# First attention of a two-layer kernel: the first two heads' convolution matrix loaded straight from a padded input, D added on its diagonal by VectorE

## The reference

```python
# head_dim 8, 16 heads over the 128 rows of the sequence axis, L = 256
kv = einsum('bhil,bhjl->bijhl', k_, v_)            # k = v = ctx
y = irfft(rfft(kv, 2L) * rfft(ssm_kernel, 2L))[..., :L]   # causal convolution along L
out = y + kv * D[None, None, None, :, None]
out = einsum('bijhl,bhil->bjhl', out, q_)          # q = layernorm(x)
x = x + out
```

## Time and profile before

| | |
|---|---|
| median of 3 runs | 797.25 us (795.12 to 798.29) |
| profiled execution, its own time | 793.92 us |
| span from its first to its last instruction | 792.2 us |
| mean granted TensorE clock | 0.960 of full speed |
| busy: PE, DVE, ACT, POOL | 709.6, 543.6, 342.7, 443.1 us |

### The profile page before, as it was taken

The page is one execution under the profiler, slowest core; times in us unless marked ns, Lnnn a source line. Parts: engine busy times, 40 slices in busy tenths (PEclk is TensorE's granted clock), DMA queues, the critical chain, the costliest instruction groups (busy, mean ns, idle before and its releaser), DMA issues.

```text
span 792.2 us, 14732 instructions
## 1 busy us (share of the span) xinstructions
PE 709.6 (90%) x5217; PEld 648.2 (82%) x5217; DVE 543.6 (69%) x1278; ACT 342.7 (43%) x698; POOL 443.1 (56%) x532
## 2 busy tenths in 40 slices
PE   4899978949999981769899999999999999999996
PEld 2444557839999970658899999999999999999996
DVE  4999988786666655676667677677676586755533
ACT  2564533235666652264354344344444534443221
POOL 5877955047666605565276466474664773443532
PEclk9999999978999995689999999999999999999998
DMA  7675516936866763414012021010020110000000
GB/s 252 191 175 123 140 41 144 195 89 194 234 197 195 164 151 125 141 54 146 1 35 61 1 60 36 14 54 28 15 67 14 34 49 1 2 14 2 2 14 14
DMA packets 44599, 68.67 MB, mean 87 GB/s; under 512 B 7376, under 2 KB 32240, under 8 KB 44528
## 3 DMA queue, kind: packets, MB, share of 16 engines
q0 software_dynamic: 10080, 28.72, 16.3%
q1 hardware_dynamic: 34352, 38.97, 15.2%
q10 hardware_dynamic: 96, 0.04, 0.0%
HBM read 50.77 MB, written 14.84 MB: 83 GB/s over the span
## 4 chain that ended last, share of the span: by engine, by line
PE 52%; DVE 4%; POOL 3%; ACT 2%; issue 2%; POOLq 0%; DVEq 0%
PE psum L1428 19%; PE psum L1413 9%; PE psum L1460 9%; PE psum L1474 4%; PE psum L1446 2%; PE psum L1510 2%; PE psum L1500 2%; PE psum L1487 2%; POOL rows_back L1699 1%; PE psum L1528 1%; PE psum L1548 1%; DVE lora_w_lo L1794 1%; PE psum L1518 1%; ACT lora_w_hi L1592 0%; POOL hid L1719 0%
## 5 line engine op out<-in xcount | busy, mean ns | idle before, releaser
L1719 POOL TENSOR_TENSOR hid<-hid,rw_sb 128x256 f32<-128x256 f32 x112 | 93.3, 833 | 153.1 <-DVE hid L1919 152.8
L1428 PE MATMUL psum<-am_hi,lora_w_hi 128*128 128x256 f32 x448 | 127.4, 284 | 2.6 <-DVE am_lo L1914 2.3
L1428 PE MATMUL psum<-am_hi,lora_w_lo 128*128 128x256 f32 x448 | 127.2, 284 | 0.0
L1428 PE MATMUL psum<-am_lo,lora_w_hi 128*128 128x256 f32 x448 | 127.1, 284 | 0.0
L1919 DVE TENSOR_TENSOR hid<-hid,psum 128x256 f32<-128x256 f32 x112 | 46.7, 418 | 116.5 <-ACT hid L1599 115.3
L1599 ACT ACTIVATE hid<-psum 128x256 f32<-128x256 f32 x112 | 42.4, 385 | 177.1 <-PE psum L1428 176.9
L1022 POOL DMA_INDIRECT rows_in<-y_scratch,slot_token x80 | 76.3, 954 | 36.0 <-issue 27.3
L1428 PEld LDWEIGHTS psum<-am_hi,lora_w_hi 128*128 128x128 f32 x448 | 86.0, 192 | 3.1 <-POOL am_lo L1730 3.1
L1699 POOL DMA_INDIRECT rows_back<-slots_scratch,comb_idx x64 | 67.1, 1049 | 37.0 <-POOLq L707 21.4
L1925 DVE TENSOR_TENSOR hid_lo<-hid,hid_hi 128x256 fp32r<-128x256 f32 x112 | 74.0, 681 | 19.3 <-ACT hid_hi L1605 14.4
L1428 PEld LDWEIGHTS psum<-am_lo,lora_w_hi 128*128 128x128 f32 x448 | 85.9, 192 | 0.0
(11 more groups left out here) (255 smaller groups left out, 2137.4 us busy)
## 6 DMA issues: line engine op xcount, KB each, us to landing
slots_scratch<-y_out SPq DMA_DIRECT2D x40, 256.0 KB, 2.5
stage<-in_moe_weights SPq DMA_DIRECT2D x18, 384.0 KB, 3.8
moe_w_lo<-in_moe_weights POOLq DMA_DIRECT2D x18, 384.0 KB, 6.5
lora_stage_early<-in_lora_weights SPq DMA_DIRECT2D x16, 384.0 KB, 3.3
x_sb<-in_x SPq DMA_DIRECT2D x4, 512.0 KB, 6.1
ctx_t<-in_ctx_t SPq DMA_DIRECT2D x4, 512.0 KB, 7.3
y_scratch<-y SPq DMA_DIRECT2D x8, 256.0 KB, 2.6
x_sb<-shared_out POOLq DMA_DIRECT2D x4, 512.0 KB, 5.2
```

Of the source, the lines that this page charges most:

```text
L1428: last = nc.tensor.matmul(x_banks[F % 2][:, w * GT:(w + 1) * GT], wp, ap, start=False, stop=(half == 1 and k == 2), skip_group_check=True)
L1719: nc.gpsimd.tensor_tensor(f[:, F % 2, k, :], f[:, F % 2, k, :], rw_sb[:, F // FB % 2, k, :], ALU.mult)\
```

## The change

The input `ssm_kernel` is padded on the host to the form of `kpad`, so that the Toeplitz block of a head can be read from it directly, without D. Part 0 (heads 0 and 1) is read in this way and no longer waits for the store; its load stands in SP's queue between the two loads of x. Parts 1 and 2 still come from `kpad_scratch`, with D in them. For heads 0 and 1 DVE adds D itself: `first_tap` is a 128 x 128 matrix with ones where the first tap stands in the block (POOL makes it: a memset and an `affine_select`), `d_first` is D of the two heads on all 128 partitions (a third DMA in ACT's queue), and two `scalar_tensor_tensor` instructions write first_tap * D + toeplitz over the block. PE's step 0 now waits for these two. POOL's two memsets of `kpad` are gone. The padded row is loaded whole (24 KB in place of 16 KB).

```diff
+    DIRECT = 2
...
-    TOEPLITZ_PARTS = ((0, 2), (2, HEADS // 2), (HEADS // 2, HEADS))
+    TOEPLITZ_PARTS = ((0, DIRECT), (DIRECT, HEADS // 2), (HEADS // 2, HEADS))
...
-                sp.dma_start(toeplitz[:, first:end, :], bass.AP(kpad_dram.tensor, first * KPAD, [
+                source = a["ssm_kernel"] if part == 0 else kpad_dram
+                sp.dma_start(toeplitz[:, first:end, :], bass.AP(source.tensor, first * KPAD, [
...
             load_x(0)
+            load_toeplitz(0)
             load_x(1)
             load_context(0)
             sp.wait_ge(kpad_stored, 16)
-            load_toeplitz(0)
             load_toeplitz(1)
...
-            nc.gpsimd.memset(kpad[:, 0:P - 1], 0.0)
-            nc.gpsimd.memset(kpad[:, P - 1 + DIM:KPAD], 0.0).then_inc(kpad_zero, 1)
             nc.gpsimd.memset(ident[:, :], 0.0).then_inc(ident_done, 1)
             nc.gpsimd.memset(minus_half[:, :], -0.5)
+            nc.gpsimd.memset(first_tap[:, :], 0.0).then_inc(tap_done, 1)
...
+            pool.wait_ge(tap_done, 1)
+            nc.gpsimd.affine_select(out=first_tap[:, :], in_=first_tap[:, :], compare_op=ALU.not_equal, fill=1.0,
+                                    base=1 - P, pattern=[[1, P]], channel_multiplier=1).then_inc(tap_done, 1)
...
-            act.dma_start(kpad[:, P - 1:P - 1 + DIM], a["ssm_kernel"]).then_inc(k_loaded, 16)
+            act.dma_start(kpad[:, :], a["ssm_kernel"]).then_inc(k_loaded, 16)
             act.dma_start(d_col[:, :], a["D"]).then_inc(k_loaded, 16)
-            act.wait_ge(kpad_zero, 1)
+            act.dma_start(d_first[:, :], a["D"][0:DIRECT, :].rearrange("h o -> (h o)").partition_broadcast(P))\
+               .then_inc(toeplitz_loaded[0], 16)
             act.wait_ge(d_added, 1)
...
-                        pe.wait_ge(toeplitz_loaded[part], 16)
+                        if part == 0:
+                            pe.wait_ge(direct_ready, DIRECT)
+                        else:
+                            pe.wait_ge(toeplitz_loaded[part], 16)
...
-            for p in range(DVE_ROWS):
-                query_rows(p)
+            query_rows(0)
+            query_rows(1)
+            dve.wait_ge(toeplitz_loaded[0], 32)
+            dve.wait_ge(tap_done, 2)
+            for h in range(DIRECT):
+                own_block = toeplitz[:, h, 0:P]
+                nc.vector.scalar_tensor_tensor(own_block, first_tap[:, :], d_first[:, h:h + 1], own_block, ALU.mult,
+                                               ALU.add).then_inc(direct_ready, 1)
+            query_rows(2)
```

More of the change, by code:

```diff
@@ L175, in first_phase @@
         prod = sb("prod", [P, HALVES * CHUNK_B, HEAD_DIM, HEAD_DIM])
-        with nc.sbuf_tensor("kpad", [HEADS, KPAD], FP32) as kpad:
+        with nc.sbuf_tensor("kpad", [HEADS, KPAD], FP32) as kpad, \
+                nc.sbuf_tensor("first_tap", [P, P], FP32) as first_tap, \
+                nc.sbuf_tensor("d_first", [P, DIRECT], FP32) as d_first:
             pass
@@ L189, in sem @@
             return s.enter_context(nc.semaphore(name))
-        kpad_zero, k_loaded, d_added, kpad_stored = map(sem, ("kpad_zero", "k_loaded", "d_added", "kpad_stored"))
+        tap_done, k_loaded, d_added, kpad_stored = map(sem, ("tap_done", "k_loaded", "d_added", "kpad_stored"))
+        direct_ready = sem("direct_ready")
         toeplitz_loaded = [sem(f"toeplitz_loaded{i}") for i in range(len(TOEPLITZ_PARTS))]
@@ L2068 @@
         "ctx_t": ctx_rev.transpose(1, 2, 0),
-        "ssm_kernel": inputs["L0_xattn_ssm_kernel"],
+        "ssm_kernel": np.pad(np.asarray(inputs["L0_xattn_ssm_kernel"]), ((0, 0), (P - 1, KPAD - DIM - P + 1))),
         "moe_gate": np.asarray(inputs["L0_ffn_gate_weight"]).T.reshape(HALVES, P, EXPERTS).transpose(1, 0, 2),
```

## The result

The changed kernel takes 799.07 us in the median of 22 runs (794.03 to 801.67), the kernel before 796.76 us (794.79 to 800.37, 22 runs). The ratio is 1.0021, 95% interval 1.0011 to 1.0031: slower by 1.7 us (0.9 to 2.5; the two medians lie 2.3 us apart), inside the 0.5% that were set as "no change", and clear of zero.

What follows compares the result with a forecast made beforehand. DVE's pace was taken to bound the step loop, so the start chain from D's landing to its first product counts; removed wait 0, additions 0, x and context 0, D +0.3 gave 797.5 us, range 794.5 to about 800.6.

Steps and rivals of the forecast that it cites:

- forecast as summed: Whole kernel: +0.3 us, to 797.5 us, with a band of -0.3 to +0.8 us; chance 0.63.
- the case "same": Whole kernel: the time changes by under 0.5% (4 us); chance 0.92, against faster 0.03 and slower 0.05.
- rival (a): DVE before pair 2: additions miss the idle hole, pair 2 waits behind POOL's kv; 0.4 to 2.5 us, likely 1.4; chance 0.22.
- The removed wait, 0: PE's step 0: Toeplitz part 0 already landed 1.8 us before PE wanted it, so dropping its wait for the store gains 0.
- DVE's additions, 0: DVE before pair 2: the two additions, 0.29 us each, fit the 0.62 us idle while POOL computes its power; cost 0.
- x and context, 0: SP's queue: the block delays x tiles 4 to 7 and the context by 1.2 us (bound 1.9), hidden by slack; cost 0.
- D, +0.3: DVE's start: D's 64-byte load lands later beside the added traffic; 0.3 us taken, bounds 0 and 1.2.
- The shift goes one to one into the total: Step loop, where DVE is 97% busy: a shift of DVE's first product reaches the kernel's end in full.
- Rival (b): Pair 2 on DVE: context lands after about 11.3, POOL's kv starts later; gain up to 1.57 us, 795.7; chance 0.04.
- (c): PE's step 0: the wait for part 0 was on the chain after all; at most 0.4 us, 796.9; chance 0.03.
- (d): Beyond the first 20 us: something unseen, such as later queues' alignment, moves the time 4 us or more; chance 0.08.
- The six-head block: Toeplitz part 1, landed at 15.8 and wanted by step 2 after 18.45: 256 KB less ahead of it, not late.

Runs made afterwards that it cites:

- run 8: The kernel before, with POOL's first kv product made to wait until DVE has written pair 2; 794.73 us, ratio 0.9983 to the kernel before.
- run 10: The changed kernel with the two-head block behind x tiles 4 to 7, D added to `kpad` after DVE's first statistics, POOL's first kv after pair 2; 793.22 us, ratio 0.9963.
- run 3: The changed kernel with the two-head block loaded behind x and the first context, and DVE's two additions behind pair 2; 796.86 us, ratio 1.0002 to the kernel before.
- run 4: The kernel before plus one extra 256 KB load of overlapping taps between the two x loads, nothing of the change; 797.97 us, ratio 1.0017.
- run 5: The kernel before plus a 256 KB load between the x loads, from separate aligned rows of x; only its start was read, x tiles 4 to 7 landing at 7.0.
- run 6: The kernel before plus a 256 KB load between the x loads, from rows of x shifted 4 bytes; only its start was read, x tiles 4 to 7 landing at 7.0.
- run 7: The kernel before plus a 256 KB load between the x loads, all partitions reading the same aligned 2 KB; only its start was read, x tiles 4 to 7 landing at 8.8.
- run 1: The changed kernel with the two-head block loaded behind x tiles 4 to 7 instead of ahead of them; 795.98 us, ratio 0.9991 to the kernel before.
- run 2: The changed kernel with the two-head block loaded behind x tiles 4 to 7 and the first context; 797.07 us, ratio 1.0001 to the kernel before.

## Why the prediction was right or wrong

The forecast was 797.5 us from a median of 797.25, a shift of +0.3; measured was 799.07 us, a shift of +1.7 us. That lies outside the band of the forecast as summed (-0.3 to +0.8), and inside the range and the case "same", by a mechanism that the sum had set to nothing. The range reached so far up only for rival (a), which did not happen; that the time fell inside it is luck. Of the prediction's own signs of being wrong one came, the idle time before the x statistics, and the first product at 20.31 missed the 18.4 to 19. Step by step:

- **The removed wait, 0:** right. PE goes from the turns into step 0 without a wait for the block in every run, though it landed at 13.1 before and at 6.2 after. (In runs 8 and 10 PE waits 0.17 us there, for kv.)
- **DVE's additions, 0:** right. They take 0.34 us each, the upper of the two rows (344 ns) and not the 0.29 that I took; they ran 11.80 to 12.41 and pair 2 started at 12.50, right behind POOL's power at 12.46. The hole was 0.1 us from too small.
- **Rival (a), the additions miss the hole:** did not happen; pair 2 began before kv (12.50 against 12.69). The two rows that the prediction set against each other, at 9.94 and at 11.29, are instructions with one tensor in SBUF; the additions, with two, were the test. The rule of the Trainium skill, SBUF — State Buffer, section Who interferes with whom, was seen for the additions where kv ran (0.69 and 1.12 us in run 3), and not beside the 4-element power (0.34 us each in the changed kernel, the power running from 11.30 to 12.46). Pair 2 behaved alike: 1.98 us beside kv, 0.41 without it (run 8: both in 0.73), 0.41 beside the power. What decides between the two was not measured.
- **x and context, 0:** this step failed. I took 216 GB/s, 1.2 us, a landing at 7.3, and called it hidden; the upper bound was 1.9. It was 2.8 us. In that place 1.8 us of 2.7 vanish when the rows come from another source, and 1.6 us of the context's 2.6 vanish when the block stands behind x. And I divided bytes by a mean rate, as if x landed once all ahead of it had moved, where 2.08 MB had moved by its landing and not 1.34. The rows had a sign of it, the 4.0 us from issue to landing that this block took on an empty queue, while twice the bytes of x took 4.8 behind another load; I used only the rates. The slack was as worked out: 1.1 us at DVE, about 0.4 at POOL, and 2.8 less both is 1.3 to 1.5, the shift of pair 2.
- **D, +0.3:** 0.1 (5.66 against 5.55), and within 0.15 of the kernel before in runs 4 to 7. In the changed kernel even this costs nothing, since DVE then waits 1.53 us for x. So the only term that the sum had above zero was not on the chain.
- **The shift goes one to one into the total:** shown up to the end of the step loop (1.86 and 1.89 us). Behind it single traces differ by more than that, and only the timed runs speak: 1.7 us (0.9 to 2.5), which agrees.
- The rest of the 1.86, 0.33 us, is PE's step 0, which no step had.
- **Rival (b)** came near by the way I had called unlikely: the context landed at 11.5, past the 11.3 named. But POOL had been moved to 12.69 by the same delay, so it saw nothing of it.
- **Rivals (c) and (d):** no sign of either. With the wait gone and x in time (run 1), PE began step 0 at 14.97, 0.12 us earlier than before, which is DVE's earlier start (5.44 against 5.55).
- **The six-head block** was to have 256 KB less ahead of it and be no later. It was 1.2 us later, by the store of `kpad`, and still in time.

## What to carry to other kernels

A load that is moved forward in a queue is paid by what it passes. Ask of each passed load when its reader wants it, and take the moved one's price from its own measured time to landing rather than from bytes over a mean rate. Here many partitions reading the same few KB of DRAM were dear in front of x, aligned or not, and cheap behind it. A load whose reader has time can stand behind the ones that are wanted first: there this one cost nothing that the timed runs show (runs 1 and 2). And where DVE and POOL meet, 1.6 us hung on pair 2's second instruction running before or beside kv (run 8), so it is worth ordering them by a wait.

## What the runs showed that I had not expected

PE's step 0 is the same work in all kernels, and its matmuls ran at two speeds. In the second experiment, from PE's timeline:

```profile
15.00 1.91 PE L457 MATMUL psum<-kv,toeplitz 128*128 128x512 f32 x2
16.71 1.55 PE L458 MATMUL psum<-kv,toeplitz 128*128 128x512 f32 x2
18.10 1.02 PE L459 MATMUL psum<-kv,toeplitz 128*128 128x512 f32 x2
```

From one pair's start to the next there are 1.71 us, then 1.39, and 0.86 later on: half speed that ends somewhere in the second pair, the ratio of the clock's two levels, 1.2 and 2.4 GHz. From the start of step 0 to the first product it was 3.36 us before the change, 3.69 after, 3.72 in run 8, 3.86 in run 1, 4.23 in run 2, 4.37 in run 3 and 4.99 in run 5. Ahead of it PE had idled 9.6 us or more, turned two pairs, idled again (not in runs 8 and 10) and turned two more. The windows' granted clock reads 1.00 throughout, so the clock as the cause is read from the durations and not shown. A start that is 0.3 us earlier can be lost again there, and since these times differ by up to 1.6 us (3.36 against 4.99), the first product's time alone measures the queue's effect no better than that. The start of DVE's second statistics does.
